# Turning the wide attention's probabilities by VectorE and DMAs in the joint last stage, and weighing a step later

## What is computed

```python
# L2, wide: 16 heads of 64 (per batch)
h = layernorm(x, gamma, beta)
Q, K, V = h @ Wq, context @ Wk, context @ Wv
attn = softmax(Q K^T) * scale
x = x + (attn @ V).reshape(NQ, 1024) @ Wo + bo
# L3, narrow: 16 heads of 8 (per batch)
q, k, v = x @ Wq^T, context @ Wk^T, context @ Wv^T
x = x + softmax(q k^T * scale) @ v @ Wo^T + bo
```

## Time and profile before

| | us |
|---|---|
| time, median of 3 runs (lowest to highest) | 1756.94 (1755.8 to 1757.06) |
| the profiled execution: its own time | 1758.43 |
| its span | 1756.3 |
| L0 stage ends, last stage begins, about | 745, 1139 |
| PE, DVE, ACT, POOL busy | 1685.5, 1340.3, 1238.9, 677.9 |

### The profile page before, as it was taken

One profiled execution on the slowest core, in us unless ns is written; L12 is line 12 of the kernel. 1 busy time (PEld: TensorE's weight loads), 2 busy tenths in 40 slices (PEclk: granted clock), 3 DMA queues, 4 the chain that ended last, 5 costly groups with the idle time before them and its releaser, 6 DMA issues. The chain is left out here.

```text
span 1756.3 us, 49692 instructions
## 1 busy us (share of the span) xinstructions
PE 1685.5 (96%) x17032; PEld 1403.7 (80%) x17032; DVE 1340.3 (76%) x2472; ACT 1238.9 (71%) x3858; POOL 677.9 (39%) x946
## 2 busy tenths in 40 slices
PE   7999999999999999889899998989999999999997
PEld 5788888788888888679677777878888888888886
DVE  5877777777777777657688886568888888888876
ACT  4777777777777777533488885457778777787786
POOL 3444444454444444323222223643433434334331
PEclk9999999999999999989999999999999999999999
DMA  6777777877677777710000000000000000000000
GB/s 183 199 190 186 186 190 191 221 208 202 188 187 186 187 191 192 200 49 0 1 1 0 0 0 1 0 1 3 7 3 3 4 3 4 3 3 4 4 6 7
DMA packets 160060, 149.18 MB, mean 85 GB/s; under 512 B 14754, under 2 KB 157668, under 8 KB 159972
## 3 DMA queue, kind: packets, MB, share of 16 engines
q1 hardware_dynamic: 159972, 148.04, 31.7%
HBM read 78.79 MB, written 69.21 MB: 84 GB/s over the span
## 5 line engine op out<-in xcount | busy, mean ns | idle before, releaser
L654 ACT ACTIVATE L_probs<-L_scores,L_neg_max 128x128 f32<-128x128 f32 x512 | 182.7, 386 | 134.6 <-DVE L_neg_max L736 134.6
L850 POOL TENSOR_TENSOR L_probs<-L_probs,L_inv_sum 128x1024 f32<-128x1024 f32 x128 | 242.8, 1897 | 88.5 <-DVE L_inv_sum L756 88.5
L730 DVE TENSOR_REDUCE L_row_max<-L_scores 128x8 f32<-128x1024 f32 x128 | 156.2, 1220 | 42.0 <-PE L_scores L530 42.0
L762 DVE STREAM_TRANSPOSE L_squares<-L_probs 128x1024 f32<-128x1024 f32 x128 | 156.7, 1224 | 0.3 <-POOL L_probs L850 0.3
L1566 ACT ACTIVATE L2L_w_probs<-L2L_scores,L2L_w_neg_max 128x128 f32<-128x128 f32 x256 | 92.0, 395 | 78.5 <-DVE L2L_w_neg_max L1724 78.5
L577 PE MATMUL L_ring<-L_probsT,L_v 128*64 128x128 f32 x2048 | 127.9, 277 | 10.0 <-issue 7.5
L577 PEld LDWEIGHTS L_ring<-L_probsT,L_v 128*64 128x64 f32 x2048 | 111.2, 137 | 30.4 <-issue 25.7
L1934 POOL TENSOR_TENSOR L2L_w_probs<-L2L_w_probs,L2L_w_inv_sum 128x1024 f32<-128x1024 f32 x64 | 121.3, 1896 | 33.1 <-DVE L2L_w_inv_sum L1760 33.1
L530 PE MATMUL L_scores<-L_kT,L_qT 64*128 64x128 f32 x2048 | 131.8, 278 | 0.9 <-ACT L_kT L643 0.9
L530 PEld LDWEIGHTS L_scores<-L_kT,L_qT 64*128 64x128 f32 x2048 | 119.4, 188 | 12.5 <-ACT L_oT L643 8.1
L746 DVE TENSOR_REDUCE L_sums<-L_probs 128x8 f32<-128x1024 f32 x64 | 78.1, 1220 | 66.1 <-ACT L_probs L661 66.1
(11 more groups left out here) (222 smaller groups left out, 4768.5 us busy)
## 6 DMA issues: line engine op xcount, KB each, us to landing
L_relay<-L_squares SPq DMA_DIRECT2D x128, 512.0 KB, 3.4
L_probsT<-L_relay SPq DMA_DIRECT2D x512, 128.0 KB, 3.7
out_x<-x SPq DMA_DIRECT2D x32, 64.0 KB, 1.5
L0a_wq<-in_L_xattn_Wq SPq DMA_DIRECT2D x2, 256.0 KB, 2.9
L0a_wk<-in_L_xattn_Wk SPq DMA_DIRECT2D x2, 256.0 KB, 3.2
L0a_wv<-in_L_xattn_Wv SPq DMA_DIRECT2D x1, 512.0 KB, 6.6
L0a_wo<-in_L_xattn_Wo SPq DMA_DIRECT2D x1, 512.0 KB, 6.7
L0b_wq<-in_L_xattn_Wq SPq DMA_DIRECT2D x1, 512.0 KB, 5.0
```

The source lines that it names most:

```text
L654: done = nc.scalar.activation(slot_probs(at, 0)[:, n, :], scores[:, 0, r, i, :], ACT.Exp, scale=layer_of(at).scale, bias=neg_max[:, n:n + ...
L730: nc.vector.tensor_reduce(row_max[:, s, :], slot(s), AX.X, ALU.max).then_inc(max_ready[s], 1)
L762: nc.vector.transpose(squares[:, at.n % 2, :, SLOT_HEADS * s:SLOT_HEADS * (s + 1), :] .rearrange("p j h a -> p h j a"), slot_probs(at, s). ...
L850: nc.gpsimd.tensor_tensor(to, to, inv_sum[:, :, s, :].unsqueeze(3) .to_broadcast([TOKENS, 2, GROUP, TOKENS]), ALU.mult).then_inc(divided, 1)
```

## The change

`w_transpose_probs` and `w_turned_probs` are gone. In their place:

- `w_turn_squares` on VectorE: one instruction per half turns the 32x32 squares of `w_probs` into `w_squares`. It waits for the division of its half and, for its target, for the DMA of the batch before.
- SyncE takes each half to DRAM with one DMA (`away`) and back with four (`back`), into `w_probsT`, which now has two buffers. SyncE's loop is unrolled, and the output DMAs stand in it at step t for batch t-4.
- `w_weigh` of batch t moves from the end of step t to step t+1, behind the wide scores; it waits for the landing.
- `w_values` and `w_weighted`, the copies of values and weighted values, move from VectorE to ScalarE.
- On TensorE `n_score` moves ahead: behind the wide output projection, before the third narrow transpose. `n_project_out` moves behind the second half of the projections.
- VectorE's, ScalarE's and GpSimd's steps are put in another order. GpSimd divides first; VectorE's `w_add_up(t+1)` now stands in the step of its scores, and `w_finish`, `n_weighted` and `n_finish` come later in the row.
- The weights of L0 are allocated last and freed after L0, to make room for the two new tiles.

```diff
-    order = [("w.q0", 2, "act"), ("w.k0", 2, "act"), ("n.T0", -3, "act"), ("n.T1", -3, "act"), ("w.Wo", -1, "dve"),
-             ("n.T2", -3, "act"), ("n.T3", -3, "act"), ("w.T0", 0, "act"), ("w.T1", 0, "act"), ("n.iT", -3, "act"),
+    order = [("w.PV0", -1, "act"), ("w.PV1", -1, "act"), ("w.q0", 2, "act"), ("w.k0", 2, "act"),
+             ("n.T0", -3, "act"), ("n.T1", -3, "act"), ("w.Wo", -1, "dve"), ("n.T2", -3, "act"), ("n.T3", -3, "act"),
...
-        w_probsT = sb("w_probsT", [TOKENS, HEADS, TOKENS])
+        w_squares = sb("w_squares", [TOKENS, SQUARES, HEADS, SQUARE])
+        w_probsT = sb("w_probsT", [TOKENS, 2, SQUARES, HEADS, SQUARE])
...
             def w_weigh(at, s):
                 await_emptied(pe, f"w.v{s}", at)
-                await_emptied(pe, f"w.T{2 * s + 1}", at)
+                w_landed(pe, at, s)
...
-                                                w_probsT[:, SLOT_HEADS * s + GROUP * r + i, :],
+                                                w_probsT[:, at.n % 2, :, SLOT_HEADS * s + GROUP * r + i, :],
...
+            def w_turn_squares(at, s):
+                dve.wait_ge(w_divided[s], at.times(1, 1))
+                if at.n >= 1:
+                    dve.wait_ge(w_relayed[s], at.times(16, 0))
+                nc.vector.transpose(w_squares[:, :, SLOT_HEADS * s:SLOT_HEADS * (s + 1), :]
+                                    .rearrange("p j h a -> p h j a"),
+                                    w_slot(at, s).rearrange("p h (j b) -> p h j b", b=SQUARE)
+                                    ).then_inc(w_squares_turned, 1)
...
             def step(t):
+                if here(t, 0):
+                    w_divide(t, 1)
                 if here(t, -1):
                     n_stage_context(t.plus(-1))
                 if here(t, 1):
+                    w_divide(t.plus(1), 0)
                     w_add_bias(t.plus(1))
...
+            def away(at, h):
+
+                sp.wait_ge(w_squares_turned, at.times(2, h + 1))
+                if at.n >= 1:
+                    w_landed(sp, at.plus(-1), h)
+                sp.dma_start(w_relay[h], w_squares[:, :, SLOT_HEADS * h:SLOT_HEADS * (h + 1), :]
+                             ).then_inc(w_relayed[h], 16)
+
+            def back(at, h):
+
+                p = at.n % 2
+                sp.wait_ge(w_relayed[h], at.times(16, 16))
+                if at.n >= 2:
+                    await_filled(sp, f"w.PV{h}", at.plus(-2))
+                for j in range(SQUARES):
+                    sp.dma_start(w_probsT[SQUARE * j:SQUARE * (j + 1), p, :, SLOT_HEADS * h:SLOT_HEADS * (h + 1), :],
+                                 w_relay[h].rearrange("(i b) j h a -> j b i h a", b=SQUARE)[j]
+                                 ).then_inc(w_probsT_landed[p][h], 16)
+
+            for t in range(first, last + 2):
+                if here(At(t), -4):
+                    await_emptied(sp, "n.Wo", At(t - 4))
+                    sp.dma_start(out_dram[:, t - 4, :], x[:, t - 4, :]).then_inc(stored, 16)
+                if here(At(t), 0):
+                    away(At(t), 1)
+                    back(At(t), 1)
+                if here(At(t), 1):
+                    away(At(t + 1), 0)
+                    back(At(t + 1), 0)
```

More of the change, by code:

```diff
@@ L1317, in n_slot, with w_landed @@
             return n_probs[:, at.n % 2, s, :, :]
+        def w_landed(engine, at, h):
+            engine.wait_ge(w_probsT_landed[at.n % 2][h], at.times(LANDED // 2, LANDED - LANDED // 2 * (at.n % 2)))
         @block.tensor
@@ L1516, in step @@
                     w_project_out(t.plus(-1))
+                if here(t, -2):
+                    n_score(t.plus(-2))
                 if here(t, -3):
@@ L1855, in step @@
                     w_normalise(t.plus(3))
+                if here(t, -1):
+                    w_finish(t.plus(-1))
                 if here(t, -2):
```

153 lines of the change are left out of this document (70 added, 83 removed).

## The result

The changed kernel took 1778.39 us (median of 4 runs, 1775.77 to 1779.41), the kernel before beside it 1757.0 (1755.8 to 1757.26): a ratio of 1.0121, 95% interval 1.0103 to 1.0138. The forecast was 1737, so it was wrong in sign. The profiled execution has a span of 1777.6 us against 1756.3. Nothing is lost to TensorE's granted clock: 0.989 over the span against 0.990 before, and 1.00 in the loop in both.

What follows compares the result with a forecast made beforehand. TensorE was taken to bound the loop: 16.55 + 0.43 + 0.65 = 17.63, taken as 17.7 us a step. Over 27 steps 16.4 less, plus 6 at the start, minus 2.3 at the end: 20.1 less, 1737 us (1717 to 1750).

Steps and rivals of the forecast that it cites:

- TensorE's own work: Last stage's loop: sixteen wide transposes leave TensorE, 1.76 us, so its work falls from 18.31 to 16.55 us a step.
- The output projection's wait: TensorE, ahead of the output projection: its ring bank waits for ScalarE's query copy, a stall of 0.43 us a step.
- The narrow weighing's wait: TensorE, ahead of the narrow weighing: it waits for the fourth narrow transpose's copy, a stall of 0.65 us a step.
- GpSimd's queue: GpSimd behind the later narrow result: division of half 1 comes to 3.8 us into the next step, hidden with 2.8 cover.
- TensorE's own rows and the loop: Step length in the last stage: TensorE's sum 17.63, taken as 17.7 us, plus 0.07 for the loop.
- B: Rival: VectorE's full row slips by 0.3 to 0.6 us, 18.0 to 18.3 a step, 1745 to 1753 us; chance 0.14.
- A: Rival: TensorE's stalls do not show; 1721 us with one stall, no lower than 1718 with neither; chance 0.14.
- C: Rival: the DMA landing ahead of half 1's weighing binds and the kernel is slower, 1783 us at 16; chance 0.06.
- D: Rival: TensorE's clock falls as it pauses twice a step; 0.95 would cost 0.8 us a step, 1759; chance 0.04.
- Both ends: First and last steps of the stage: step 3 begins about 6 us earlier, the end comes 2.3 us later.

Runs made afterwards that it cites:

- c2: Changed kernel with seven edits: c1's four, copies ahead only from step 3, normalised rows also ahead of the inverse, more reordering on TensorE, GpSimd and VectorE; 1708.17 us.
- e1: Changed kernel, with GpSimd waiting for VectorE's negated wide maxima before it divides half 1; 1752.05 us, ratio 0.9973 to the kernel before.
- e2: Changed kernel, with the wide maxima negated by ScalarE instead of VectorE and GpSimd's division left in place; 1752.12 us, ratio 0.9982 to the kernel before.
- c1: Changed kernel with four edits: division behind the negation, ScalarE's query and key copies ahead, normalised rows ahead of the statistics, narrow weighing later; 1751.29 us.
- r2: Kernel before, with unneeded GpSimd multiplications added in each step behind the negated wide maxima; 1756.85 us, ratio 1.0005 to the kernel before.
- d1: Changed kernel, with half 1's squares sent first to a spare place in DRAM, a longer way; 1785.43 us, ratio 1.0164 to the kernel before.
- c3: c2 without GpSimd's wait for the negated maxima before dividing half 1; 1710.86 us, ratio 0.9738 to the kernel before.
- e3: Changed kernel, with ScalarE copying the first queries and keys ahead of its second four wide exponentials; 1777.99 us, ratio 1.0126 to the kernel before.
- e4: Changed kernel, with VectorE writing the normalised rows behind the inverse of half 0 and ahead of the statistics; 1779.70 us, ratio 1.0137 to the kernel before.
- e5: Changed kernel with the edits of e3 and e4 together; 1768.47 us, ratio 1.0079 to the kernel before.
- r1: Kernel before, with unneeded GpSimd multiplications added in each step so that they run at the negation; 1789.38 us, ratio 1.0197 to the kernel before.

## Why the prediction was wrong, step by step

**What bounds, TensorE's own work: right.** 16.55 a step; c2 has 16.57 where it has no wait. Turning the probabilities elsewhere did free 1.76.

**The output projection's wait: right in place, wrong in size.** 0.43 of idle time forecast, 1.30 measured in that step (1.2 on average in the loop), and TensorE got there at 7.08 instead of 6.65. The step that failed is the sentence "ScalarE's first exponential starts at 1665.24 - 1662.56 = 2.68, as now, since it hangs on scores and maxima". It hangs on the negated maxima. In the changed kernel it starts at 3.87. e1 and e2, with the negation free, have 2.7, and the wait is 0.37 and 0.41 in the steps named above.

**The narrow weighing's wait: right.** 0.65 forecast, 0.68 measured.

**GpSimd's queue: here the prediction had the cause in hand.** It worked out that `n_add_bias` moves behind the late narrow result and that the division of half 1 "comes to about 21.5, that is 3.8 into the next step", which is its end: measured 3.81 (3.5 and 3.9 in turn in the loop). It then asked only who waits for the division's result ("hidden, with 2.8 us of cover"), and not which of VectorE's instructions meet it. The negation at 2.46 lies in its middle. A few lines above, the same lock had been found in the earlier trace rows and put into VectorE's row for the normalised rows (1.75 forecast; 1.75 and 1.55 in turn in the loop). The rule had been applied to the place where a row of the trace showed it and not to the place to which the change moved the division.

The Trainium skill, "SBUF — State Buffer", section "Who interferes with whom", has the rule: a `tensor_scalar` that uses both port pairs and a GpSimd instruction shut each other out for a whole instruction, by whichever is first, while a `tensor_reduce` is never held. The runs agree: 128x8 in 0.17 us held up to 1.46; c1's rows first 0.34, second 1.86; and the reductions beside r2's added work, which kept their 1.2 us.

**TensorE's own rows and the loop: too short, and it mattered.** Outside the loop a step of e1 takes 17.96 where I had 17.7, with VectorE's rows held for 1.75 (steps 3 and 27) and with rows of 0.29 and no statistics (step 28) alike; step 4, which leads into the loop, takes 18.14. The narrow result ends there at 17.03, within my 17.25. What was short is TensorE's sum: 17.96 less its waits of 0.38 and 0.68 is 16.90, not 16.55. Its rows beside a wait are longer than in a full row. Inside the loop e1's step is 18.34, 0.38 more, and I had let the loop add 0.07. There VectorE's row is too short as well: the narrow result ends at 1523.24 - 1505.80 = 17.44 in one step of a turn and at 17.74 in the other, and TensorE's next fill follows it. The traces show 0.27 of idle time without a releaser ahead of the scores once a turn, and pauses of 0.1 to 0.2 in VectorE's row that the steps outside do not have. What makes them is open. Timelines of e1, VectorE, the narrow result in the step from 1505.80, then the rows and the narrow result in step 28, from 1651.83:

```profile
1522.95 0.29 DVE L1823 TENSOR_TENSOR x<-L2L_ring,L2L_n_x_bias 128x128 f32 x1
...
1659.70 0.29 DVE L1722 TENSOR_SCALAR L2L_w_rows_h<-x,L2L_moments,L2L_rstd 128x128 f32<-128x128 f32 x1
...
1668.61 0.25 DVE L1823 TENSOR_TENSOR x<-L2L_ring,L2L_n_x_bias 128x128 f32<-128x128 f32 x1
```

Together it is 18.26 against 17.77, 13 us of the whole. So of the 1.43 by which the changed step missed the forecast, 0.94 is the negation (e1 against the changed kernel) and 0.49 is this.

**Rivals.** B was the right kind ("each us that its instructions lose to GpSimd ... goes into the step whole"), but was priced at 0.3 to 0.6, without the instruction that would lose it. A: with the stalls gone TensorE was to be held by VectorE near 17.2, not under 1718 us; c2, with other orders on all four engines, gave 16.82 and 1708. C and D: shown out by d1 and by the clock.

**Both ends.** The first steps were to give 6 and gave 4.7, or 5.1 with the earlier start; the end was to cost 2.3 and cost 4.1. In c2 and c3, where the last weighing goes ahead of the narrow scores, it is 55.6 and 57.9 against 57.2 before.

## What to carry to other kernels

When a change moves a long GpSimd instruction, in code or only in time, lay its new interval over VectorE's row and look for every `tensor_scalar` in it, however small: its price isn't its own length but the rest of the GpSimd instruction, and where nothing behind it has slack each step pays it whole. The runs show this for `tensor_scalar` only: the reductions and the subtraction from PSUM beside r2's added work kept their 1.2 us, and no experiment was made on VectorE's other instructions. Put such an instruction ahead of the one that lets GpSimd go, or hand it to ScalarE. And an edit that gains nothing alone isn't yet judged: where two chains run through the same late result, each hides the other.

## What the runs showed of the hardware

A negation of 8 numbers in each of 128 partitions, 0.17 us alone, takes 0.35 to 1.47 us when it starts inside a GpSimd multiplication of 128x1024 that takes 1.90: whatever it has left. In the 210 such cases of the seven traces that have them (the changed kernel, d1, e3, e4, e5, c3 and r1) the negation ended 0.03 us behind the multiplication. With VectorE first, the GpSimd instruction lost almost nothing (1.93 against 1.90). ScalarE did the same negation in 0.21 in the middle of the division. The way of half the probabilities to DRAM and back took 3.5 and 2.9 us from issue to landing, with 112 GB/s going on (DMA issues of the changed kernel: KB each, median us):

```profile
L2L_relay<-L2L_w_squares SPq DMA_DIRECT2D x64, 512.0 KB, 3.5
L2L_w_probsT<-L2L_relay SPq DMA_DIRECT2D x256, 128.0 KB, 2.9
```
